# Expert rows added to the output by accumulating scatters, weighed in ScalarE's copy

## The reference

```
x = x + xattn(layernorm(x), ctx)     # 16 heads of 32, context of 16 x 1601 rows
x = x + linear_attn(layernorm(x))    # elu(q)+1, elu(k)+1, sums over the sequence
x = x + moe(layernorm(x))            # 8 experts, each token takes its best 2
# moe: probs = softmax(x @ router.T); w, sel = top_k(probs, 2)
#      h = x @ w1[e].T (512 -> 2048); y = h[1024:] * silu(h[:1024])
#      out[token] = sum over its two experts e of w_e * (y @ w2[e].T)
```

## Time and profile before

| | us |
|---|---|
| median of three timed runs (lowest, highest) | 2516.41 (2516.23, 2518.18) |
| the profiled execution | 2518.01 |
| its span in the trace | 2516.3 |
| PE busy in the span | 2366.8 (94%) |
| DVE, ACT, POOL busy | 1296.1, 1086.3, 1076.6 |
| mean granted PE clock | 0.974 |

### The profile page before, as it was taken

How to read it: one execution, slowest core, us unless ns; L and a number is a source line. 1 busy time by engine, 2 the same in 40 slices (tenths; PEclk the granted TensorE clock), 3 DMA queues, 4 the chain that set the end, 5 groups by cost and what they waited for, 6 DMA issues and landing times. The chain is left out here.

```text
span 2516.3 us, 41241 instructions
## 1 busy us (share of the span) xinstructions
PE 2366.8 (94%) x14585; PEld 2092.1 (83%) x14585; DVE 1296.1 (52%) x2185; ACT 1086.3 (43%) x1865; POOL 1076.6 (43%) x439
## 2 busy tenths in 40 slices
PE   8999999999999999999999999999658958999985
PEld 7798998889899889989988998988527738999875
DVE  3245555555455555555545555555654465555544
ACT  3354544445444444444545454544412214444432
POOL 2255555555555555555555555555520021111114
PEclk9999999999999999999999999999879979999998
DMA  4311121221112121111212111123040034444444
GB/s 154 104 41 47 45 60 41 62 56 41 48 45 59 41 65 52 41 48 45 65 37 70 47 41 48 45 74 99 7 159 1 18 113 143 151 151 151 141 149 155
DMA packets 150050, 186.13 MB, mean 74 GB/s; under 512 B 79552, under 2 KB 108224, under 8 KB 149824
## 3 DMA queue, kind: packets, MB, share of 16 engines
q1 hardware_dynamic: 144192, 168.76, 21.7%
q0 software_dynamic: 2560, 8.39, 1.0%
q10 hardware_dynamic: 3072, 6.03, 0.6%
HBM read 139.29 MB, written 43.84 MB: 73 GB/s over the span
## 5 line engine op out<-in xcount | busy, mean ns | idle before, releaser
L399 POOL TENSOR_TENSOR k_parts<-k_t,k_parts 64x1602 fp32r<-64x1602 f32 x128 | 426.1, 3329 | 448.9 <-DVE k_parts L464 448.8
L719 PE MATMUL ps_kv<-ctx_hi,wk_hi 128*128 128x256 f32 (+1 forms) x1536 | 463.3, 302 | 9.1 <-DVE ctx_lo L578 7.6
L719 PE MATMUL ps_kv<-ctx_lo,wk_hi 128*128 128x256 f32 (+1 forms) x1536 | 441.2, 287 | 0.0
L719 PE MATMUL ps_kv<-ctx_hi,wk_lo 128*128 128x256 f32 (+1 forms) x1536 | 441.1, 287 | 0.0
L510 DVE TENSOR_TENSOR probs_t<-ps_pt,probs_t 128x512 fp32r<-128x512 f32 x368 | 205.9, 559 | 445.9 <-ACT probs_t L629 443.6
L413 POOL TENSOR_TENSOR v_parts<-v,v_parts 128x832 fp32r<-128x832 f32 x128 | 283.3, 2213 | 335.3 <-ACT v_parts L647 333.8
L719 PE MATMUL ps_kv<-wv_hi,ctx_hi 128*128 128x512 f32 (+1 forms) x832 | 340.9, 410 | 0.0
L719 PE MATMUL ps_kv<-wv_hi,ctx_lo 128*128 128x512 f32 (+1 forms) x832 | 327.9, 394 | 0.0
L719 PE MATMUL ps_kv<-wv_lo,ctx_hi 128*128 128x512 f32 (+1 forms) x832 | 327.1, 393 | 0.0
L617 ACT ACTIVATE k_t<-ps_kv,bk_sb 128x256 f32<-128x256 f32 (+1 forms) x384 | 185.6, 484 | 310.9 <-PE ps_kv L719 307.5
L719 PEld LDWEIGHTS ps_kv<-ctx_hi,wk_hi 128*128 128x128 f32 x1536 | 292.0, 190 | 12.5 <-issue 10.0
(11 more groups left out here) (275 smaller groups left out, 4113.4 us busy)
## 6 DMA issues: line engine op xcount, KB each, us to landing
w_raw<-w_dram SPq DMA_DIRECT2D x96, 512.0 KB, 4.9
ctx_raw<-ctx_dram SPq DMA_DIRECT2D x81, 512.0 KB, 3.9
rows_in<-zeros SPq DMA_DIRECT2D x150, 128.0 KB, 3.6
ctx_raw<-ctx_dram SPq DMA_DIRECT2D x16, 644.0 KB, 5.6
q_blocks<-q_parts SPq DMA_DIRECT2D x256, 32.0 KB, 1.9
rows<-rows_in SPq DMA_DIRECT2D x8, 768.0 KB, 6.2
rows_out<-zeros SPq DMA_DIRECT2D x1, 5376.0 KB, 17.7
rows_out<-down ACTq DMA_DIRECT2D x7, 768.0 KB, 3.6
```

Of the source, the lines that this page charges most:

```text
L399: nc.gpsimd.tensor_tensor(k_parts[64 - 64 * s:128 - 64 * s, :], k_t[par][64 * s:64 * s + 64, g, :], k_parts[64 * s:64 * s + 64, :].bitcast ...
L719: last = nc.tensor.matmul(o, still, moving, start=(k == 0 and i == 0), stop=(k == DT - 1 and i == 2))
```

## The change

Six edits are in the diff.

1. `rows_out`, its zeroed tail, the gathers, the weighing on VectorE and the stores at the end are gone, with `combine_places` and half of `combine_weights`.
2. A table `slips` in HBM holds for every place of `rows_in` a token number and a weight (8 bytes). It is first filled with spare token numbers (1024 to 1535) and weight 0, and then 16 indirect scatters on GpSimd write the true slips, after the weights are known. The output tensor has 512 spare rows.
3. SP stores x2 to the output in slot 0 (2 MB, and 1 MB more to the spare rows), before w1 block 4. In u = 6 of each slot it loads the slot's 384 slips, ahead of w1 block 6; in slot 0 it first waits for all 16 slip scatters, later for the scatters of slot s-2.
4. ScalarE's copy of a second-layer bank multiplies by the slip's weight, and GpSimd adds the rows to the output by an accumulating indirect scatter, 128 rows each: three for a slot, two for the last. One slot's scatters wait until those of the slot before have landed, and the next copy to `down` waits for them.
5. w2 is loaded from ScalarE's queue: block 0 after silu of u = 0, blocks 1 to 3 after silu of u = 1, 3, 5. SP loads slot 0's rows after w1 block 1 instead of block 3.
6. In routing steps t > 8 `choose` and `assign` work on the tile of the step before, ahead of the head work and the projection, and there is one step more. At the start of the program wv_hi is made after the second bank is emptied instead of before the first.

```diff
+            def load_slips(s, par):
+                if is_first(s):
+                    sp.wait_ge(slips_stored, 16 * 2 * TT)
+                row = sp.value_load(slot_row[0:1, bass.ds(s, 1)], min_val=0, max_val=E * REGION)
+                if positive(s - 1):
+                    sp.wait_ge(added, 16 * RB * (s - 1))
+                sp.dma_start(slot_slips[par][:], slips[bass.ds(row, BLOCK), :].rearrange("(r p) c -> p r c", p=P)
+                             ).then_inc(slips_loaded, 16)
...
-                    if u == RAW and is_first(s):
+                    if u == AHEAD and is_first(s):
                         sp.wait_ge(dispatched, 16 * 2 * TT)
                         sp.wait_ge(tables_done, 2)
                         load_rows(0)
                     if u == IT // 2 and not last:
                         load_rows(s + 1)
+                    if u == RAW and is_first(s):
+                        ov = out[0:NT, :].rearrange("(t p) d -> p t d", p=P)
+                        sp.dma_start(ov, x2[:]).then_inc(x_stored, 16)
+                        sp.dma_start(out[NT:, :].rearrange("(t p) d -> p t d", p=P), x2[:, 0:SPARE // P, :]).then_inc(x_stored, 16)
+                    if u == IT - 2:
+                        load_slips(s, par)
...
-                    if u % WC == WC - 1:
...
-                        if positive(k - 1):
-                            sp.wait_ge(w2_lo_done, k - 1)
-                        sp.dma_start(w2_raw[c % 2][:], w2[bass.ds(e, 1), c].rearrange(
-                            "a p (k n) -> (a p) k n", k=WC)).then_inc(w2_loaded[c % 2], 16)
...
+            def add_rows(s, par, tiles):
+                pool.wait_ge(down_free, RB * s + tiles)
+                if is_first(s):
+                    pool.wait_ge(x_stored, 32)
+                else:
+                    pool.wait_ge(added, 16 * RB * s)
+                if positive(s):
+                    pool.wait_ge(marked, s)
+                nc.gpsimd.tensor_tensor(added_mark[:], ident[:, 0:1], ident[:, 1:2], ALU.subtract).then_inc(marked, 1)
+                for r in range(tiles):
+                    nc.gpsimd.indirect_dma_start(
+                        out=out, out_offset=bass.IndirectOffsetOnAxis(ap=slot_slips[par][:, r, 0:1], axis=0),
+                        in_=down[:, r, :], in_offset=None, compute_op=ALU.add).then_inc(added, 16)
...
+                if not is_first(s):
+                    add_rows(s - 1, 1 - par, RB)     # after the four w2 blocks of slot s
...
+            pool.wait_ge(combine_ready, 1)
+            pool.wait_ge(spare_stored, 16)
+            for r in range(TT):
+                for j in range(2):
+                    nc.gpsimd.indirect_dma_start(
+                        out=slips, out_offset=bass.IndirectOffsetOnAxis(ap=place[:, r, j:j + 1], axis=0),
+                        in_=slip[:, r, j, :], in_offset=None).then_inc(slips_stored, 16)
             last = over_slots(pool, slot)
+            add_rows(last, 1, LAST_RB)
+            pool.wait_ge(added, 16 * (RB * last + LAST_RB))
...
-            def store_down(s, tiles):
+            def weigh_down(s, par, tiles):
                 act.wait_ge(parts_done, IT * (s + 1))
+                act.wait_ge(slips_loaded, 16 * (s + 1))
                 if positive(s):
-                    act.wait_ge(down_stored, 16 * s)
+                    act.wait_ge(added, 16 * RB * s)
                 for r in range(tiles):
-                    nc.scalar.copy(down[:, r, :], ps_d[r][:]).then_inc(down_free, 1)
...
+                    nc.scalar.activation(down[:, r, :], ps_d[r][:], ACT.Copy, scale=slot_slips[par][:, r, 1:2].bitcast(F32)
+                                         ).then_inc(down_free, 1)
...
+                    if u == 0:
+                        if first:
+                            act.wait_ge(tables_done, 1)
+                        e = act.value_load(slot_expert[0:1, bass.ds(s, 1)], min_val=0, max_val=E - 1)
+                        load_w2(s, e, 0)
+                    if u % WC == WC - 1 and u // WC + 1 < NW2:
+                        load_w2(s, e, u // WC + 1)
```

In the routing steps the order changes like this (VectorE above, TensorE below; the removed calls stood at the end of the step):

```diff
+                if t > TT:
+                    choose(t - 1 - ROUTE)      # after finish_rows, before the head work
...
+                elif t > TT:
+                    assign(t - 1 - ROUTE)      # before start_rows
-                if t >= TT:
-                    choose(t - ROUTE)
-                    assign(t - ROUTE)
...
+                if t > TT:
+                    rank(t - 1)                # before the projection
-                if t >= TT:
-                    rank(t)
```

More of the change, by code:

```diff
@@ L669, in _ @@
             for kind, k in start_steps():
+                if kind == "unit" and k == 2:
+                    act.wait_ge(wv_loaded, 16)
+                    nc.scalar.copy(wv_hi[:], wv_raw).then_inc(w_hi_done, 1)
                 if kind == "unit":
@@ L1132, in attend_route_and_experts @@
         w2_hi, w2_lo, y_hi, y_lo, down = (m.at[n] for n in ("w2_hi", "w2_lo", "y_hi", "y_lo", "down"))
-        taken = xn
-        stored_mark = sb("stored_mark", [P, 2])
+        token = sb("token", [P, TT, 2], I32)
+        added_mark = sb("added_mark", [P, 1])
+        slip = sb("slip", [P, TT, 2, 2], U32)
+        spare_at = sb("spare_at", [P, SLIPS], I32)
+        spare = sb("spare", [P, SLIPS, 2], U32)
+        slot_slips = [sb(f"slot_slips{i}", [P, RB, 2], U32) for i in range(2)]
         ps_pair = [mem.enter_context(nc.psum_tensor(f"ps_pair{i}", [P, 2, BANK], F32)) for i in range(2)]
@@ L1166, in attend_route_and_experts @@
         combine_ready = sem("combine_ready")
+        spare_made, spare_stored, slips_stored, slips_loaded = (
+            sem("spare"), sem("spare_stored"), sem("slips_stored"), sem("slips_loaded"))
+        x_stored, added, marked = sem("x_stored"), sem("added"), sem("marked")
         dispatched = sem("dispatched")
@@ L1174, in attend_route_and_experts @@
         up_done, silu_done, y_done, y_hi_done, y_lo_done = sem("up"), sem("silu"), sem("y"), sem("y_hi"), sem("y_lo")
-        parts_done, down_free, down_stored = sem("down_parts"), sem("down_free"), sem("down_stored")
-        taken_done = [sem(f"taken{i}") for i in range(TT)]
-        weighed, stored, all_stored = sem("weighed"), sem("stored"), sem("all_stored")
+        parts_done, down_free = sem("down_parts"), sem("down_free")
         block = mem.enter_context(nc.Block())
@@ L1529, in combine_weights @@
                 then(nc.vector.reciprocal(total[:], total[:]))
-                then(nc.vector.tensor_tensor(share[:], lifted[:, :, E:E + 2], total[:].unsqueeze(2).to_broadcast([P, TT, 2]),
-                                             ALU.mult))
-                for j in range(2):
-                    then(nc.vector.tensor_tensor(cross[:, :, j, 0], share[:, :, j], kept[:], ALU.mult))
-                    then(nc.vector.tensor_tensor(cross[:, :, j, 1], share[:, :, 1 - j], swapped[:], ALU.mult))
-                nc.vector.tensor_reduce(weight[:], cross[:], AX.X, ALU.add).then_inc(combine_ready, 1)
+                nc.vector.tensor_tensor(slip[:, :, :, 1].bitcast(F32), lifted[:, :, E:E + 2],
+                                        total[:].unsqueeze(2).to_broadcast([P, TT, 2]), ALU.mult).then_inc(combine_ready, 1)
             def slot(s, par, last, width):
@@ L1574, in _ @@
                                                    in1=expo[r % 2][:], op0=ALU.max, op1=ALU.add).then_inc(mapped, 1)
-            dve.wait_ge(pool_consts, 7)
+            dve.wait_ge(pool_consts, 9)
             nc.vector.tensor_copy(before[:], triangle[:]).then_inc(rank_consts, 1)
             nc.vector.tensor_copy(ones[:], all_ones[:]).then_inc(rank_consts, 1)
+            nc.vector.tensor_copy(slip[:, :, :, 0], token[:])
+            then(nc.vector.tensor_scalar(spare_at[:], spare_at[:], SPARE - 1, NT, ALU.bitwise_and, ALU.bitwise_or))
+            nc.vector.memset(spare[:, :, 1], 0).then_inc(spare_made, 1)
+            nc.vector.tensor_copy(spare[:, :, 0], spare_at[:]).then_inc(spare_made, 1)
             nc.vector.tensor_scalar(taken_before[:, 0, :], lane[:], float(REGION // P), None, ALU.mult).then_inc(counted, 1)
@@ L1656, in _ @@
             slot_tables()
-            combine_places()
             for u in range(AHEAD):
@@ L1664, in _ @@
             rest_y(end_slot, IT - 1, WIDTH[-1])
-            for k in range(2):
-                for t in range(TT):
-                    n = TT * k + t
-                    dve.wait_ge(taken_done[t], 16 * (k + 1))
-                    if n:
-                        dve.wait_ge(weighed, n)
-                    nc.vector.scalar_tensor_tensor(out=x2[:, t, :], in0=taken[:, t, :], scalar=weight[:, t, k:k + 1],
-                                                   in1=x2[:, t, :], op0=ALU.mult, op1=ALU.add).then_inc(weighed, 1)
         @block.tensor
```

113 lines of the change are left out of this document (27 added, 86 removed).

## The result

| | before | after |
|---|---|---|
| median, us (lowest to highest, runs) | 2516.41 (2514.39 to 2524.80, 7) | 2507.78 (2503.50 to 2511.19, 7) |
| the profiled execution, its span | 2518.01, 2516.3 | 2511.19, 2509.4 |

The ratio is 0.9956, 95% interval 0.9944 to 0.9968: 0.4% faster, 8.6 us. The forecast was 25.9 us, and 2507.8 lies above its range. The trace after is of the slowest of the seven executions, and its span is 6.9 us shorter than the one before.

The account below looks back on a forecast made before the run. Inside the slots only lost TensorE time was to be won, with SP waiting for w2. Terms -11.0 - 15.6 - 1.5 + 1.9 + 0.3 = -25.9 us gave a profiled 2492.1, median 2490.5; range 2482 to 2506.

Parts of the forecast that it names:

- into slot 0: Way into slot 0: earlier rows' gain lost to the slips, w1 block 6 1.5 us early; -1.5, bounds -5 and +8.
- signs of being wrong: Listed: L over 7 us in DMA issues; TensorE gaps in slots 1 to 6; w1 blocks landing over 8 us after issue.
- Rival B: Slot 0 breaks: slip scatters, stores and rows queue up, w1 block 6 leaves 8 us late; 2500; chance 0.16.
- w2 on ScalarE's queue: Slots: SP's w2 waits vanish, 8.0 us of TensorE waits and 3.0 at the lower clock go; 11.0 us won.
- Rival A: Slots: w1 starving stays because loads still share the DMA engines; 2501.5; chance 0.17.
- The end: After the last products: accumulating scatters replace gathers, weighing and stores; end at 2500.7, 15.6 us before 2516.3.
- L: Time from an accumulating scatter's issue to its landing, put at 4.9 us, between 2.8 and 6.9.
- Routing: Routing steps: step 9 gains 0.7, later ones lose; net +1.9 us, other bound -5.7.
- Start: Program start: wv_hi moves behind the second bank's copy, first value product waits; +0.3 us, bounds -1 and +1.9.

Follow-up runs that it names:

- e3: Kernel before, with only the 3 MB of stores added ahead of w1 block 4 in slot 0: median 2520.09 us, ratio 1.0013 to 1.0032.
- e6: Kernel before, with both the 3 MB of stores and 16 scatters of 8-byte rows added in slot 0: median 2529.01 us, ratio 1.0042 to 1.0070.
- e7: Kernel before, with the 3 MB of stores and 16 scatters of 512-byte rows added in slot 0: median 2522.52 us, ratio 1.0024 to 1.0044.
- e1: Changed kernel, with the x2 stores moved ahead of slot 0's first w1 load: median 2499.30 us, ratio 0.9919 to 0.9945.
- e5: Kernel before, with only 16 scatters of 8-byte rows added in slot 0, nobody waiting there: median 2522.17 us, ratio 1.0017 to 1.0037.
- e12: Changed kernel, with slot 0's slips loaded behind w1 block 7, stores left in place: median 2506.45 us, ratio 0.9951 to 0.9978.
- e8: Changed kernel, with x2 stores ahead of slot 0's first w1 load and its slips behind w1 block 7: median 2490.79 us, ratio 0.9892 to 0.9922.
- e9: The e8 kernel with the old routing order and wv_hi again ahead of the first bank: median 2493.21 us, ratio 0.9899 to 0.9931.
- e4: Changed kernel, with choose, assign and rank back at the end of their routing steps: median 2503.82 us, ratio 0.9936 to 0.9964.

## Why the prediction was wrong

- **The step that failed is "into slot 0", priced at -1.5.** It holds rows that come earlier (16.34 us of waiting fell to 11.55, 4.8 won, as put) and slot 0 itself (+18.2). Together +13.4 (18.2 less 4.8): off by 14.9 of the 19.0 us by which the span missed its forecast. The working said that the stores "take 10 us, and block 4 lands near 2090". I took a rate from a lone 5376 KB transfer under cross attention (311 GB/s) and gave it to stores that ran beside 16 scatters of 8-byte rows. With the stores alone that holds: in e3 block 4 landed at 2091.24. Beside the scatters all DMA engines together moved 179 to 212 GB/s, and block 4 landed at 2107.79, 18 us later than put. e6 against e7 shows, in the kernel before, that the short rows lengthen it; e1 shows that 12 us go with the stores. One of my own signs of being wrong was there: a w1 block that lands over 8 us after its issue (29.4).
- **The 8-byte rows were weighed at the wrong place, and too low.** I asked only when each slip lands, 2.8 us after its issue, or 2.1 later by the rule of the Trainium skill ("DMA: Bandwidth & Descriptors", Specifications), and not what it takes from the transfers beside it. That, as e6 against e7, is 6.2 us of slot 0. The landing was wrong too: the median is 3.7 us for scatters alone (e5), 8.5 beside the stores (e6) and 10.1 in e12, and SP, which I had held to about 2093, was held to 2106.90. It was hidden, as e12 shows, because block 4 was later still.
- **Rival B** named the right place ("scatters, stores and rows queue up") but the wrong link. It had w1 block 6 behind the slips, which e12 shows to be hidden, and 9.5 us.
- **w2 on ScalarE's queue, -11.0:** right. 13.0 between the two traces, 9.2 against the mean of the four other kernels with the old slots. Rival A, which the Trainium skill ("DMA: Bandwidth & Descriptors", Issuing engines are not separate DMA queues) would have favoured, is out: what went was the wait ahead of the issue.
- **The end, -15.6:** measured -12.3 from TensorE's last product on. L was 5.2 for 4.9 at this place; in e8's trace it is 4.7 to 7.4. I had left the pitch at 1.28 (it is 1.87) and the weighed copies at 1.07 (1.27, so the scale is not quite free); landing by landing: +0.6 to slot 6's landing, +0.9 from there to the last issue (3.1 put, 4.01 measured), +1.75 from that to the end (5.3 put, 7.05 measured), which makes 3.3.
- **Routing, +1.9:** right in size. 2.4 between the two traces and 2.5 between e9 and e8, but 0.9 between e4 and the changed kernel; it stays on the path up to the rows' turn.
- **Start, +0.3:** not resolved. The copy moved as put (13.24, near 13.5), but what it is worth does not show. VectorE's fourth rounding of ctx begins at 36.13 before and 36.59 after, but at 35.8 to 38.4 in others, with either order.
- **What is left open:** e6 explains 11.1 of slot 0's 18.2 us. The changed kernel has two w2 blocks in the same stretch (issued at 2084.71 and 2091.51, their 4 KB packets at 339 to 644 ns on average, 160 usual), and no kernel took these away alone. Nor did one widen the slips in the changed kernel itself. Nor was it found why builds differ by up to 9 us before linear attention.

## What to carry to other kernels

Price a transfer at the rate of a stretch with the same neighbours: 16 scatters of 8-byte rows by themselves lengthened the landing of two w1 blocks by 2 to 4 us (e5), but with 3 MB of stores beside them the DMA engines moved 221 GB/s instead of 366. So move bulk stores out of their stretch (e1, 12 us of slot 0); wider rows helped in the kernel before (e7) and are untried in the changed one. Count also what a scatter holds up on the engine that issues it: that alone cost 4.8 us of slot 0 in e5. When you take a long wait out of an in-order queue, list the waits that stand behind it; the second shows only when the first is gone. And cut the traces at the same instructions before you judge an edit by medians of different builds.

## What the runs showed that I had not expected

- 8-byte scattered rows beside 3 MB of stores: DMA share 1.10 at 221 GB/s, block 4 landed after 21.2 us (e6); 512-byte rows: 0.88 at 340, 15.1 us (e7).
- A scatter of 128 rows of 8 bytes lands after 3.7 us by itself and after 8.5 beside the stores (medians of e5 and e6).
- An accumulating scatter of 128 rows of 2 KB: GpSimd 1.56 us (plain 0.97), pitch 1.87 (plain 1.30), landing 4.7 to 7.4 us (e8).
- One build starts linear attention at 1900.3 and 1901.1, the others at 1891.9 to 1896.9, with the same code in cross attention.
- The same matmuls (41 in each trace) behind a wait of 12 us: 9.30 us at a granted clock of 0.83 in e8, 11.65 us at 0.60 in e9.
